# Keys split into two fp16 parts by POOL from an fp32 copy, the context fetched earlier in the queue, and the context normalised in two POOL operations instead of twelve

## The reference

```python
# layer 1 (layer 2 the same without the condition's scale and bias; layer 3 with no norm of the context)
h    = (ctx - mean(ctx)) / sqrt(var(ctx) + eps)          # per context row, over 128 features
xkv  = (1 + scale)[:, None, :] * h + bias[:, None, :]    # scale, bias from the condition
q    = (xq @ Wq + bq).reshape(16, 56, 16, 8)
k, v = split(xkv @ Wkv + bkv)                            # each 16, 1500, 16 heads, 8
attn = softmax(einsum('bqhd,bkhd->bhqk', q, k) / sqrt(8))
out  = einsum('bhqk,bkhd->bqhd', attn, v)
x    = x + out @ Wp + bp
```

## Time and profile before

| what | value |
|---|---|
| median of 3 runs | 2054.87 us (2048.06 to 2065.39) |
| profiled execution, its own time | 2056.51 us |
| its span, first to last instruction | 2054.7 us |
| PE busy | 1635.4 us (80%) |
| DVE busy | 1236.0 us (60%) |
| ACT busy | 1004.1 us (49%) |
| POOL busy | 422.9 us (21%) |
| mean granted TensorE clock | 0.892 of full speed |

### The profile page before, as it was taken

The page is one execution under the profiler, slowest core; times in us unless marked ns, Lnnn a source line. Parts: engine busy times, 40 slices in busy tenths (PEclk is TensorE's granted clock), DMA queues, the critical chain, the costliest instruction groups (busy, mean ns, idle before and its releaser), DMA issues.

```text
span 2054.7 us, 53923 instructions
## 1 busy us (share of the span) xinstructions
PE 1635.4 (80%) x20495; PEld 1030.7 (50%) x20495; DVE 1236.0 (60%) x2433; ACT 1004.1 (49%) x1911; POOL 422.9 (21%) x611
## 2 busy tenths in 40 slices
PE   4788777588887887787688888887785888888876
PEld 3465544255555555443355555555342455555554
DVE  5454443567775776364677777773364777777762
ACT  1243322166665666242366666663242466666662
POOL 7000133013331333135033333310131000000000
PEclk9798988599998998796699999996796799999997
DMA  5021122234443442040344444430040444444410
GB/s 174 26 77 64 45 44 62 55 82 112 112 110 94 113 102 73 1 103 3 72 112 113 111 109 111 110 98 14 0 102 11 92 116 117 114 114 112 106 43 9
DMA packets 178537, 166.32 MB, mean 81 GB/s; under 512 B 67551, under 2 KB 168098, under 8 KB 178402
## 3 DMA queue, kind: packets, MB, share of 16 engines
q1 hardware_dynamic: 176818, 163.35, 30.2%
q10 hardware_dynamic: 1008, 1.05, 0.2%
q0 software_dynamic: 576, 0.02, 0.0%
HBM read 114.46 MB, written 40.08 MB: 75 GB/s over the span
## 4 chain that ended last, share of the span: by engine, by line
PE 64%; issue 13%; DVE 10%; ACT 10%; DMA 1%; POOL 1%; ACTq 0%; DVEq 0%; SPq 0%; POOLq 0%
PE PS L1127 11%; PE PS L1022 8%; PE PS L1153 8%; PE PS L1016 8%; PE PS L862 6%; PE PS L1101 5%; PE PS L1011 3%; PE PS L941 3%; ACT q_parts L795 2%; DVE mx L1552 2%; PE PS L1227 2%; PE PS L959 2%; ACT v_sb L729 2%; ACT cxT L720 2%; PE PS L932 1%
## 5 line engine op out<-in xcount | busy, mean ns | idle before, releaser
L1552 DVE TENSOR_REDUCE mx<-PS 112x1 f32<-112x500 f32 x1152 | 718.4, 671 | 295.8 <-PE PS L1101 291.5
L795 ACT ACTIVATE q_parts<-PS 125x448 f32<-125x448 f32 x1152 | 562.2, 544 | 108.8 <-PE PS L1153 105.0
L585 POOL TENSOR_SCALAR cx<-cx,norm_b 125x128 f32<-125x128 f32 x384 | 303.5, 813 | 590.7 <-DMA cx<-in_ctx 488.2
L1153 PE MATMUL PS<-q_st,k_st 50*125 50x112 f16 x4608 | 263.1, 236 | 40.1 <-ACT q_parts L795 23.2
L1153 PEld LDWEIGHTS PS<-q_st,k_st 50*125 50x125 f16 x4608 | 186.4, 140 | 213.7 <-ACT q_parts L795 121.7
L1101 PE MATMUL PS<-k_st,q_mx 50*112 50x500 f16 x1152 | 262.5, 403 | 38.8 <-issue 24.2
L1127 PE MATMUL PS<-q_parts,v_sb 125*18 125x112 f32 x9216 | 291.4, 270 | 0.0
L1127 PEld LDWEIGHTS PS<-q_parts,v_sb 125*18 125x18 f32 x9216 | 218.4, 101 | 60.7 <-issue 52.1
L729 ACT ACTIVATE v_sb<-PS 125x512 f32<-125x512 f32 x144 | 87.1, 605 | 186.7 <-PE PS L1022 186.6
L725 ACT ACTIVATE k_hi<-PS,vec 128x500 f16<-128x500 f32 x144 | 97.5, 677 | 129.0 <-PE PS L1016 129.0
L1101 PEld LDWEIGHTS PS<-k_st,q_mx 50*112 50x112 f16 x1152 | 91.5, 133 | 74.5 <-issue 44.9
(11 more groups left out here) (266 smaller groups left out, 1994.1 us busy)
## 6 DMA issues: line engine op xcount, KB each, us to landing
k_st<-k_dram SPq DMA_DIRECT2D x864, 62.5 KB, 2.2
cx<-in_ctx SPq DMA_DIRECT2D x56, 750.0 KB
k_dram<-k_hi SPq DMA_DIRECT2D x144, 125.0 KB, 1.8
k_dram<-k_lo SPq DMA_DIRECT2D x144, 125.0 KB, 2.0
v_sb<-in_ctx SPq DMA_DIRECT2D x8, 750.0 KB
q_mx<-q_all SPq DMA_DIRECT2D x48, 99.8 KB
q_st<-q_all SPq DMA_DIRECT2D x48, 99.8 KB
q_all<-q_dram SPq DMA_DIRECT2D x18, 196.0 KB, 6.4
```

The costliest lines, as they stand in the source:

```text
L585: last = pool.tensor_scalar(cx[:, p, c, :], cx[:, p, c, :], norm_b[:, p, 0, c:c + 1], norm_b[:, p, 1, c:c + 1], ALU.subtract, ALU.mult)
L795: act.activation(probs[:, c % RING, u * HR:(u + 1) * HR], PS[0:KC, (2 * c + u) % SC_RING, 0:HR], ACT.Exp).then_inc(sem("exp_done"), 1)
L1153: last = mm(PS[0:KC, (2 * c + a) % SC_RING, k * PW:k * PW + PW], k_st[64 * a:64 * a + ROWS, p, k, c * KC:(c + 1) * KC], q_st[64 * a:64 * a ...
L1552: dve.tensor_reduce(mx[:, r, t:t + 1], PS[0:PW, MX_BANK + u % MX_RING, 0:TK], AX.X, ALU.max)\
```

## The change

Four things change, and a buffer.

1. ACT reads a K step out once, into a new fp32 tile `k_full` with two buffers. PE's next step waits for that alone. POOL then makes `k_hi` (a cast) and `k_lo` (a subtraction of `k_hi` from `k_full`) from SBUF. DVE's `k_low` is gone everywhere, also in the MLP of layer 1 and in the self attentions.
2. For the first two batches of each cross attention POOL does the six splits (`split_first`) after all its `self_copies`, or in layer 1 after the normalisation of batches 0 and 1.
3. SP's `load` stands ahead of `k_out` and `k_in` in an attend instead of behind them.
4. The normalisation is two POOL operations on the whole 125 x 1536 tile, with mean and deviation as broadcast operands.

The ring of exponentials (`RING`) also shrinks from 6 chunks to 4.

```diff
-RING = 6
+RING = 4
...
+        k_full = sb("k_full", [128, 2, S])
...
                         q_max(behind)
+                        if not (isinstance(b, int) and b + 4 >= B):
+                            load((b + 4, i + 2, p))
                         k_out(behind, 0)
                         k_in(behind, 0)
                         k_out(behind, 1)
                         k_in(behind, 1)
                         k_out(behind, 2)
-                        if not (isinstance(b, int) and b + 4 >= B):
-                            load((b + 4, i + 2, p))
...
+            def split_keys(layer, batch, t):
+                b, i, p = batch
+                n = B * (layer - 1) + b
+                cols = slice(TK * t, TK * t + TK)
+                ge_known(pool, ("k_full_done", NT * n + t + 1), (f"k_out{t}", 32 * n))
+                pool.tensor_copy(k_hi[:, cols], k_full[:, p, cols]).then_inc(sem("k_hi_done"), 1)
+                ge_known(pool, ("k_hi_done", NT * n + t + 1))
+                pool.tensor_tensor(k_lo[:, cols], k_full[:, p, cols], k_hi[:, cols], ALU.subtract)\
+                    .then_inc(sem("k_lo_done"), 1)
+
+            def split_first(layer):
+                for b in range(2):
+                    for t in range(NT):
+                        split_keys(layer, (b, 0, b), t)
...
-                    for c in range(C):
-                        last = pool.tensor_scalar(cx[:, p, c, :], cx[:, p, c, :], norm_b[:, p, 0, c:c + 1],
-                                                  norm_b[:, p, 1, c:c + 1], ALU.subtract, ALU.mult)
-                    last.then_inc(sem("cx_normed"), 1)
+                    pool.tensor_tensor(cx[:, p, :, :], cx[:, p, :, :], mean, ALU.subtract).then_inc(sem("norm_copied"), 1)
+                    ge_known(pool, ("norm_copied", 3 * (n0 + b + 1)))
+                    pool.tensor_tensor(cx[:, p, :, :], cx[:, p, :, :], rstd, ALU.mult).then_inc(sem("cx_normed"), 1)
...
                     if third and cr["norm"] is not None:
                         copies(third)
                         normalise(third)
+                    if behind:
+                        for t in range(NT):
+                            split_keys(layer, behind, t)
...
                 self_copies(2)
+                split_first(2)
                 cross_copies(2, True)
...
-                        ge(act, f"k_out{t}", 32 * n)
-                        act.activation(k_hi[:, TK * t:TK * t + TK], PS[:, bank, 0:TK], ACT.Identity, bias=cr["kb"])\
-                           .then_inc(sem("k_hi_done"), 1)
+                        ge(act, "k_lo_done", NT * (n - 2) + t + 1)
+                        act.activation(k_full[:, p, TK * t:TK * t + TK], PS[:, bank, 0:TK], ACT.Identity, bias=cr["kb"])\
+                           .then_inc(sem("k_full_done"), 1)
...
-                            pe.wait_ge(sem("k_hi_done"), NT * n + wt + 1)
-                            pe.wait_ge(sem("k_lo_done"), NT * n + wt + 1)
+                            pe.wait_ge(sem("k_full_done"), NT * n + wt + 1)
...
-                        if behind and not of_next:
-                            k_low(behind, k)
```

More of the change, by code:

```diff
@@ L592, in cross_copies @@
                     if cr["norm"] is not None:
-                        copies((0, 0, 0))
-                        copies((1, 0, 1))
-                        normalise((0, 0, 0))
-                        normalise((1, 0, 1))
+                        for b in range(2):
+                            copies((b, 0, b))
+                            normalise((b, 0, b))
                     return
@@ L623, in _ @@
                 self_copies(3)
+                split_first(3)
                 cross_copies(3, True)
@@ L1444, in l0_last @@
                 l0_evidence(b)
-            def preparation(layer):
-                cr = cross_of(layer)
-                n0 = B * cr["n"]
-                def k_low(batch, k, bank=MISC_BANK):
-                    kind, t = MISC[k]
-                    if kind != "K":
-                        return
-                    b, i, p = batch
-                    n = n0 + b
-                    dve.wait_ge(sem("k_hi_done"), NT * n + t + 1)
-                    ge(dve, f"k_out{t}", 32 * n)
-                    cols = slice(TK * t, TK * t + TK)
-                    dve.scalar_tensor_tensor(out=k_lo[:, cols], in0=PS[:, bank, 0:TK], scalar=cr["kb"],
-                                             in1=k_hi[:, cols], op0=ALU.add, op1=ALU.subtract)\
-                       .then_inc(sem("k_lo_done"), 1)
-                return k_low
             l0_batches(l0_first, l0_both, l0_last, dve)
@@ L1493, in _ @@
             for k in range(2 * E + 1):
-                if layers > 1:
-                    ahead(k_low, AHEAD[3 * k:3 * k + 1], DENSE_BANK)
                 dve.wait_ge(sem("hid_tanh"), k + 1)
@@ L1502, in _ @@
                                          op0=ALU.add, op1=ALU.mult).then_inc(sem("hid_done"), 1)
-                if layers > 1:
-                    ahead(k_low, AHEAD[3 * k + 1:3 * k + 3], DENSE_BANK)
                 if k == 1:
@@ L1544, in cross @@
                     last.then_inc(sem("q_split"), 1)
-                k_low = preparation(layer)
                 def unit(batch, u):
@@ L1675, in both @@
                     front(n)
-                    ahead(k_low, beside[0:1], SELF_BANK)
                     back(b)
-                    ahead(k_low, beside[1:3], SELF_BANK)
                 batches(dve, front, both, back)
```

7 lines of the change are left out of this document (3 added, 4 removed).

## The result

The changed kernel takes 2002.09 us (median of 4 runs, 1994.79 to 2009.87), the kernel before 2059.76 us beside it: ratio 0.9728, 95% interval 0.966 to 0.9796. It is 2.7% faster, and 66 us slower than forecast. The profiled execution took 1994.79 us (span 1993.0) against 2056.51 (2054.7).

The account below looks back on a forecast made before the run. PE was taken to be bound by waits for DVE's `k_lo` in the cross attentions. 2056.5 - 124 + 5 - 8 - 3 + 2 + 9 = 1937.5, less 1.6 for the median: 1936 us, range 1905 to 1990.

Parts of the forecast that it names:

- Earlier fetch. Worth 0 by itself: SP's context load ahead of the key stores: no gain by itself, its possible cost left to a rival; 0 us.
- nobody waits for POOL's context: POOL's 488.2 us of waiting for the context was taken as idle time of an engine nobody waits for.
- The rival on it: Cross attentions: the fetch, issued ahead of the key stores, delays the keys; +25 to +40 us, about 1968 us, chance 0.10.
- the 113 forecast: Cross attentions: gain in us from K steps and clock, less small waits and POOL beside DVE (124 + 3 - 5 - 9).
- The argument from the DMA share of 0.39: Against the late-keys rival: DMA share is only 0.39 to 0.40, so the engines have room for fetch and keys.
- K steps read out once, -124: Cross attentions: PE waits only for ACT's read-out, no longer DVE's `k_lo`; 2.96 us for each of 42 attends, -124 us.
- Clock, -3: Cross attentions: fewer gaps may raise PE's granted clock; -3 us (0 to -15).
- POOL's new work, 0: POOL's splits, at most 5.6 us an attend, and two normalisations, 5.8 us, hold nobody up; 0 us.
- POOL beside DVE, +9 (0 to 65): Attend ends in layers 1 and 2: POOL's long normalisation holds DVE's `msplit`; 0.35 us for some 26 attends, +9 us.
- The first two batches, +2 (0 to 8): Turn into layer 3: splits and key transfers after the self attention make `stack_q` 1.7 us late; +2 us.
- If the transfers also queue: Turn into layer 3: condition for the upper end, +8 us, of the first two batches' term.
- The rest of the self attentions and the MLP, -8: Outside the cross attentions: half of the 16 us of K and V0 waits goes; -8 us (0 to -16).

Follow-up runs that it names:

- e6: The changed kernel with the fetch late, behind the third key store, and POOL splitting the three key tiles before normalising the context: 1952 us, ratio 0.9512.
- e1: The changed kernel with only the context fetch put back behind the third key store of each attend: 2110 us.
- e8: The changed kernel whose early fetch brings only one of twelve context columns from the fifth batch on, the others keeping stale numbers: 1920 us.
- e4: The changed kernel with the context normalisation in its twelve small POOL operations again, early fetch kept: 1991.6 us.
- e5: The changed kernel with the first two batches' key splits in layers 2 and 3 placed among POOL's self-attention copies: 1977.8 us.
- e2: The kernel before with only the fetch moved ahead of the key stores on SP's queue: same time within 0.3%.
- e3: The changed kernel with the early fetch issued on ACT's DMA queue instead of SP's: 1989.6 us.
- e12: e9 with its late fetch issued on ACT's DMA queue, behind ACT's read-out of K2, instead of SP's: 2003.6 us.
- e10: e9 with the fetch in three pieces of 250 KB, one ahead of each key store of an attend: 2104 us.
- e9: e6 with the first two batches' splits among the self attention's copies, as in e5: 1947.8 us, ratio 0.9437.

## Why the prediction was wrong

**The step that failed is "Earlier fetch. Worth 0 by itself".** The changed kernel's three cross attentions take 42 us more (1104.6) than those of e6 (1062.1), which has the fetch behind the keys and, so that this can work, the splits ahead of the normalisation. Layer 3, where POOL has no normalisation and e1 therefore changes the place of the fetch alone, gives 10 to 13 us by e1 and 15 by e6. That is most of the 50 us that are missing there; e6 itself stays 7 us short of the 113 forecast. I also said that nobody waits for POOL's context, which was true of the earlier trace rows and false as soon as the same change put the key splits behind it: with the fetch late and nothing else changed the kernel takes 2110 us (e1).

The rival on it named the right mechanism and gave it 25 to 40 us and a chance of 0.10, so what I had wrong is mostly the chance. It had the landing right as well, a store that lands only behind the fetch: 10.5 us after the fetch's issue there, 8.8 to 10.1 in the trace. Three things are missing in it, which the runs show. The fetch does not leave 4 us ahead of the store but within 1.5 us of its second half in 20 of the 36 attends, since SP has lost its slack. SP's round then sets the pace. And the wait was priced at its length, where PE's clock falls behind it: of the 75 us between the changed kernel and e8, 42 are idle time and 33 slower matmuls. The argument from the DMA share of 0.39 against the rival was no argument: a mean share says nothing about one small transfer behind one large one.

**K steps read out once, -124.** About right. All terms for the cross attentions come to 113. With the whole fetch behind the keys (e6) they take 105.9 us less than before, with eleven twelfths of it gone (e8) 137.9 less, and e8 drops work that the kernel before has. One attend of 37.1 us in layer 1 before had no counterpart in e8. There the attend is 22.0 to 23.6 us in the steady part, about as written.

**Clock, -3.** Wrong sign in the changed kernel: 0.96, 0.93 and 0.95 in the three windows, after 0.96, 0.96 and 0.99. It is 0.97, 0.99 and 0.98 in e8. The clock followed the waits.

**POOL's new work, 0.** The durations were right: cast and subtraction take 609 + 1139 ns, 1.75 us where I had at most 1.9, and the normalisation 2753 + 2794 ns, 5.5 us where I had 5.8. The figure that I worked out from the Trainium skill (GPSIMD Engine Reference, Performance versus the Vector engine), an estimate of 3.4 us, is too high by a fifth against the 2.75 us of the trace.

**POOL beside DVE, +9 (0 to 65).** Mechanism right, in layers 1 and 2 alone, with 23.5 us of PE's waits in the profile; but e4 shows the same time for the cross attentions without it, since PE then waits for the keys instead. Where the keys are not late it may cost something: 10.9 us of PE's waits in e8. The rule of the Trainium skill (SBUF — State Buffer, Who interferes with whom) that the two exclude each other for a whole instruction agrees with the 2.65 us here. But the step held is 21 times of 23 the first, with one SBUF input, not the one with two on which I had built; the same section of the Trainium skill counts `tensor_scalar` among those that can do so.

**The first two batches, +2 (0 to 8).** The lateness was found and under-sized: +9.1 for the turn. Some 5 of it are that `q_dram` lands 7 us after its issue and not 2; the rest is that it is issued later, where I had 1.7 us. "If the transfers also queue" was the right doubt, and the measured value lies just above its range. e5 takes 13 us off.

**The rest of the self attentions and the MLP, -8.** The start up to the first cast takes 409.2 us before and 408.7 in e2, and 400.5 to 403.3 in the six profiles of kernels whose POOL does the same work in the same order up to there (the changed one and its repeat, e1, e3, e5 and e8): 6 to 9 us less. The turn from layer 1 to 2 did not gain (196.8 us, then 196.7), and the turn into layer 3 can't be read for it. So about the term's 8 us came in all, from one place instead of three.

## What to carry to other kernels

A wait that costs nothing is a property of what stands behind it: before moving work to an idle engine, list what that engine waits for, and place the new work ahead of those waits. In this kernel the bulk transfer did best right behind the last small transfer of the latency chain, not ahead of it, and neither another queue (e12) nor smaller pieces (e10) replaced that; even there it cost some 32 us against e8. Once a wait is removed, compare the round of every in-order sequencer (here SP's 25 us) with the new length of the loop, not the old one.

## What the runs showed of the hardware

- A store of 2 x 125 KB that leaves up to 5.1 us behind a transfer of 750 KB lands 8.8 to 10.1 us after that transfer's issue (changed kernel, 36 attends; e2, 8.7 to 10.0). On average it takes 6.4 us instead of 2.0 (longest 9.0); behind a fetch from the other queue 7.0 (e12, second tile, longest 8.9). 250 KB ahead of it cost 2.0 to 2.4 us (e10).
- After a 750 KB transfer was issued, the issue of a store half from SP, 0.34 us as a rule, took up to 4.09 us 4 to 7 us later (e3), and up to 3.09 us 8 us later (e9).
- Behind a wait of PE of 4.8 us its granted clock was at 0.50 for about 10 us (0.57, 0.50 and 0.65 in three stretches of 4 us). The attend was 8.3 us longer than the same one in e8.
- A `tensor_scalar` of DVE on 8 elements per partition took 2.65 us beside a POOL operation of 2.75 us.
